# Splitting a unit's last attention tile before or after the next queries, on ScalarE and VectorE

## The reference

```python
q, k, v = layernorm(x) @ Wq, ...                 # 16 query heads, one key head, one value head
sim = jnp.einsum('bhid,bjd->bhij', q, k) + bias  # a null column stands in front
sim = jnp.where(causal_mask, neg, sim)
attn = jax.nn.softmax(sim, axis=-1)
out = jnp.einsum('bhij,bjd->bhid', attn, v)
out = out.transpose(0, 2, 1, 3).reshape(b, n, INNER) @ Wo
x = x + layernorm(out)
```

## Time and profile before

| what | value |
|---|---|
| median of 3 runs | 1648.43 us (1646.07 to 1648.87) |
| the profiled execution, its own time | 1648.25 us |
| span of the profiled execution | 1646.4 us, so 1.85 us lie around it |
| attention, first to last L1210 | about 52 to 1303 us of the span |
| TensorE, VectorE, ScalarE, GpSimd busy | 88%, 85%, 70%, 51% of the span |

### The profile page before, as it was taken

One profiled execution on the slowest core, in us unless ns is written; L12 is line 12 of the kernel. 1 busy time (PEld: TensorE's weight loads), 2 busy tenths in 40 slices (PEclk: granted clock), 3 DMA queues, 4 the chain that ended last, 5 costly groups with the idle time before them and its releaser, 6 DMA issues.

```text
span 1646.4 us, 44788 instructions
## 1 busy us (share of the span) xinstructions
PE 1441.4 (88%) x15551; PEld 1064.3 (65%) x15551; DVE 1406.3 (85%) x3562; ACT 1150.6 (70%) x2957; POOL 838.8 (51%) x1654
## 2 busy tenths in 40 slices
PE   3567778888999999986788899999999989999998
PEld 2445556666777777765666677777777756666665
DVE  5467787899999999987788899999999979888887
ACT  3466667887888888877788888888999723333332
POOL 4768687664554545457775443433232266632222
PEclk8589899999999999999999999999999999999999
DMA  4011121220222213111221212222214001000000
GB/s 147 19 31 55 40 65 53 84 67 33 79 79 91 91 58 125 59 40 33 72 78 53 85 66 72 79 85 91 98 65 144 2 4 43 1 1 1 14 14 26
DMA packets 50754, 96.46 MB, mean 59 GB/s; under 512 B 3732, under 2 KB 27364, under 8 KB 50532
## 3 DMA queue, kind: packets, MB, share of 16 engines
q1 hardware_dynamic: 47988, 92.65, 17.2%
q10 hardware_dynamic: 2544, 0.94, 0.3%
HBM read 91.41 MB, written 2.17 MB: 57 GB/s over the span
## 4 chain that ended last, share of the span: by engine, by line
PE 54%; DVE 21%; issue 7%; ACT 6%; POOL 5%; DVEq 0%; ACTq 0%; POOLq 0%
PE tp L1728 8%; DVE biased L1210 7%; PE sc L1606 5%; DVE p_lo L1309 5%; PE sc L1407 4%; PE sc L1409 4%; PE sc L1408 4%; PE sc L1607 4%; DVE q_a L1242 3%; PE aux L1407 3%; PE op L1407 2%; PE aux L1409 2%; PE aux L1408 2%; PE tp L1407 2%; PE tp L1409 2%
## 5 line engine op out<-in xcount | busy, mean ns | idle before, releaser
L1309 DVE TENSOR_TENSOR p_lo<-tp,p_hi 128x384 f16<-128x384 f32 (+3 forms) x768 | 413.1, 553 | 90.1 <-ACT p_hi L902 80.7
L805 ACT ACTIVATE probs<-biased,neg_max 128x256 f32<-128x256 f32 (+7 forms) x512 | 395.2, 772 | 25.9 <-DVE neg_max L1210 23.7
L1728 PE MATMUL tp<-ident,probs 128*128 128x128 f32 x2304 | 389.7, 278 | 2.4 <-DVE p_lo L1309 1.8
L902 ACT ACTIVATE p_hi<-tp 128x384 f16<-128x384 f32 (+3 forms) x768 | 369.4, 491 | 28.1 <-PE tp L1728 14.3
L1606 PE MATMUL sc<-k_a,q_a 128*128 128x512 f16 (+3 forms) x768 | 254.6, 332 | 90.3 <-DVE neg_max L1210 70.6
L1407 PE MATMUL op<-v_s,p_hi 128*128 128x64 f16 x2304 | 285.2, 194 | 42.7 <-DVE p_lo L1309 27.4
L1728 PEld LDWEIGHTS tp<-ident,probs 128*128 128x128 f32 x2304 | 266.8, 142 | 29.0 <-issue 10.7
L1409 PE MATMUL op<-v_s,p_lo 128*128 128x64 f16 x2304 | 284.2, 194 | 0.0
L1408 PE MATMUL op<-v_s,p_hi 128*128 128x64 f16 x2304 | 284.2, 194 | 0.0
L1407 PEld LDWEIGHTS op<-v_s,p_hi 128*128 128x128 f16 x2304 | 215.6, 98 | 71.7 <-DVE p_lo L1309 48.6
L1607 PE MATMUL sc<-k_b,q_b 128*128 128x512 f16 (+3 forms) x768 | 242.5, 329 | 0.0
(11 more groups left out here) (311 smaller groups left out, 3508.6 us busy)
## 6 DMA issues: line engine op xcount, KB each, us to landing
bias<-rel_table SPq DMA_DIRECT2D x4, 2048.0 KB, 8.0
bias<-in_fside_16xSxS SPq DMA_DIRECT2D x4, 2048.0 KB, 8.6
bias<-rel_table SPq DMA_DIRECT2D x4, 1792.0 KB, 7.8
bias<-in_fside_16xSxS SPq DMA_DIRECT2D x4, 1792.0 KB, 7.1
bias<-rel_table SPq DMA_DIRECT2D x4, 1536.0 KB, 7.6
bias<-in_fside_16xSxS SPq DMA_DIRECT2D x4, 1536.0 KB, 6.7
bias<-rel_table SPq DMA_DIRECT2D x4, 1280.0 KB, 5.8
bias<-in_fside_16xSxS SPq DMA_DIRECT2D x4, 1280.0 KB, 6.5
```

The costliest lines, as they stand in the source:

```text
L805: ac.activation(probs[:, i % 2, 0:w], biased[:, i % 2, 0:w], ACT.Exp, bias=neg_max[:, u % 2, i % HU:i % HU + 1], scale=-1.0, accum_out=row ...
L902: ac.activation(p_hi[:, gi % 4, 0:nb * P], tp[gi % 2][:, 0:nb * P], ACT.Copy)\
L1309: ve.tensor_tensor(p_lo[:, gi % 4, 0:nb * P], tp[gi % 2][:, 0:nb * P], p_hi[:, gi % 4, 0:nb * P], ALU.subtract).then_inc(s["p_lo"], 1)
L1728: last = te.transpose(tp[gi % 2][:, jj * P:(jj + 1) * P], probs[:, n % 2, (j0 + jj) * P:(j0 + jj + 1) * P], ident[:, :])
```

## The change

In a unit's last slot (k = 3) ScalarE and VectorE do the work on the queries of unit m + 2 later. Before, ScalarE's two copies to `q_b` and VectorE's two subtractions into `q_a` stand ahead of the slot's first group of probabilities. Now they stand behind the first group and ahead of what is left of the slot: with one group, behind all of the slot's probabilities; with two, between the two groups. The waits that the instructions carry are the same, and so are the instructions themselves and their number. TensorE's, GpSimd's and SyncE's lists are the same.

```diff
@@ ScalarE, before the slot's groups
-                if k == 3 and 0 <= m + 2 < NU:
-                    u = m + 2
-                    act.wait_ge(s["q_t"], u + 1)
-                    if u >= 2:
-                        act.wait_ge(s["scores"], HU * (u - 1))
-                    for e in range(2):
-                        ac.activation(heads(q_b[0:DH, u % 2, :], e),
-                                      first[e * DH:(e + 1) * DH, 0:UW].rearrange("p (c q) -> p c q", q=P), ACT.Copy)\
-                            .then_inc(s["q_hi"], 1)
+                def queries():
+
+                    u = m + 2
...
@@ ScalarE, in the loop over the slot's groups, behind p_hi of group j
                     if j == 0:
+                        if k == 3 and 0 <= m + 2 < NU:
+                            queries()
                         small()
```

More of the change, by code:

```diff
@@ L838, in _ @@
                         .then_inc(s["q_na"], 1)
+                def queries():
+                    u = m + 2
+                    act.wait_ge(s["q_t"], u + 1)
+                    if u >= 2:
+                        act.wait_ge(s["scores"], HU * (u - 1))
+                    for e in range(2):
+                        ac.activation(heads(q_b[0:DH, u % 2, :], e),
+                                      first[e * DH:(e + 1) * DH, 0:UW].rearrange("p (c q) -> p c q", q=P), ACT.Copy)\
+                            .then_inc(s["q_hi"], 1)
                 def small():
```

## The result

| | before | changed |
|---|---|---|
| median | 1648.25 us (1646.07 to 1648.87, 4 runs) | 1683.39 us (1682.39 to 1683.96, 4 runs) |
| span of the profiled execution | 1646.4 us | 1682.0 us |
| TensorE's granted clock, mean | 0.973 | 0.974 |

The changed kernel is slower: the ratio is 1.0215, 95% interval 1.0197 to 1.0233. The forecast was 1680 us.

The account below looks back on a forecast made before the run. A loop of waits between TensorE, ScalarE and VectorE, not one full engine, was taken to bound the kernel. Long steps 23.5 us plus short steps 8.8 gave 32 us on 1648.25: 1680 us, range 1660 to 1700.

Parts of the forecast that it names:

- The loop in the long steps: Low half, y, TensorE's queue to k = 1's transposes, `p_hi`, VectorE's list, next low half: later y lengthens the unit.
- What was forecast to come back: Unit 114: of y's 0.84 us delay, 0.17 returns at the transposes behind y and 0.09 at the next slot's first scores.
- Its size: Long steps' cost: 56 of 64 units at 0.42 us, 23.5 us in all, bounds 9.5 and 37 us.
- The eight stretches with the rows' statistics: One long unit per step has next rows' statistics before the low half; TensorE already waits at y, so counted as nothing.
- Through which wait it comes back to VectorE: Long steps: the delay returns through VectorE's wait for `p_hi` in k = 1, idle 0.29 us before, as long or longer after.
- the rival of the late queues: Long steps: y's copy on ScalarE delays the next `p_hi`, another 0.3 us, 0.9 a unit at most; about 1698 us; chance 0.14.
- The short steps: Next `biased` up to 0.28 us later, TensorE's scores wait for it: 7 us layer 1, 1.8 layer 0, 8.8 together.
- the quarter: Layer 0's 28 short units taken at a quarter of layer 1's cost, 1.8 us, as their chain holds more than this loop.
- The waits moved as told: Short steps: TensorE's wait for `p_lo` falls near zero, that for `neg_max` grows by about as much.
- the rival of the faster short steps: Short steps: TensorE's 12.9 us wait for `p_lo` paces them and goes, as much again in layer 0; 1632 us; chance 0.08.
- The hidden case: VectorE is the bound and TensorE's slack hides y's delay: 0 to 9.5 us in long steps, about 1653 us; chance 0.12.
- The loop in k = 1: Long steps: VectorE idles 0.29 us for `p_hi`, whose transposes TensorE reaches after y, products, scores and query projection.

Follow-up runs that it names:

- experiment 5: Changed kernel with y and ScalarE's copy of it moved behind the first group's transposes and products in k = 0 of the long steps: 1664.67 us.
- experiment 4: Kernel before with the new order in VectorE's list alone, ScalarE's list in the old order: 1715.0 us, ratio 1.0409.
- e1_long_only: Kernel before with the new order only in slots with two groups (long steps), the old order elsewhere: 1671.12 us, ratio 1.0139.
- experiment 11: Kernel before with the query projection of k = 1 between first transposes and products, only in one-group slots (short steps): 1633.37 us, ratio 0.9916.
- experiment 7: Kernel before with the query projection and ScalarE's copies of it behind the first group's transposes and products in k = 1, everywhere: 1695.4 us.
- experiment 12: Kernel before with the query projection between first transposes and products in k = 1, except in three slots per tile step: 1633.51 us, ratio 0.9918.

## Why the prediction was right, and where it was not

**The loop in the long steps: right.** y starts 0.05 us behind the low half, the wait for `q_a` went from 12.2 to 31.9 us (25 to 35 forecast), and experiment 5, which takes y out of the way and leaves the rest of the change, takes 17 of 24 us back. In unit 114 the low half ends 0.75 us later (0.84 forecast: the copies start 0.11 us before `p_hi` ends by its record, and I had put them behind it, so the low half waits for `p_lo` and not for them). What was forecast to come back came back: on the chain the transposes behind y end at 1189.60 + 0.44 - 31.01 = 1159.03 against 1158.45, 0.58 us later, and the first scores behind them at 1160.22 against 1159.74, 0.48 later. So the two terms are 0.17 and 0.10 (0.17 and 0.09 forecast), and the unit pays 0.75 - 0.27 = 0.48, not the 0.58 of the prediction; that VectorE's next pass behind `o_raw` is 0.58 us later too (1192.20 - 31.01 = 1161.19 against 1160.61) is chance, since one slot on it is 0.49.

**Its size: right, by terms that were each a little off and made up for each other.** Forecast 56 units of 0.42 us and eight of nothing, 23.5; measured 23.7. The eight stretches with the rows' statistics grew too, by 0.19 to 0.40 us, 2.1 in all: the wait for the statistics does not hide the whole of the later low half. Why, no run shows; `p_lo` now stands ahead of the low half there too. The other 56 took 21.6 / 56 = 0.39. Layer 0's long steps cost less than layer 1's (10.5 against 13.2), as said.

**Through which wait it comes back to VectorE: the step that failed.** I expected VectorE's idle time in k = 1 as long or longer. It is shorter, 0.20 us against 0.29, and a new one of 0.33 stands in k = 0, where there was none. It is so in all long steps, not in this unit alone: by the rows of the timeline VectorE's wait for `p_hi` in tile steps 12 to 15 went from 1.1 us (3 times) to 9.4 (25 times) in k = 0 and from 4.9 (20 times) to 1.5 (7 times) in k = 1, and in tile steps 4 to 7 from 0.8 to 7.1 and from 8.5 to 5.8. That is the rival of the late queues: y's copy ends at 1190.03 and the first `p_hi` behind it at about 1190.68, where the rival, with the shift, had 1190.11 and 1190.73. Its mechanism is there and its price is not: the longer wait in k = 0 shortens the one in k = 1, and the unit pays 0.49, not 0.9. Where ScalarE's queue is really late it does cost, as experiment 4 showed.

**The short steps: the sum near, its shares not.** Forecast 7 us in layer 1 and 1.8 in layer 0; measured 6.0 and 4.85. Layer 1's term was priced by unit 78, whose next pass is 0.14 us later and not 0.28, again because the copies overlap the end of `p_hi` (they start at 843.66, 0.10 before it). At 0.14 a unit the sum would have been 4 us, so that it came near is luck; and 1.3 of the 6.0 us lie in tile step 9, which is as much longer in `e1_long_only` with the old order. In layer 0 the quarter was a guess with no row behind it; 3.5 of its 4.85 us lie in tile step 3, most of them in two units (0.89 and 1.39). I can't say from the runs what these two wait for. The waits moved as told, in part: that for `p_lo` fell from 12.9 to 5.4 us and not to near zero, and that for `neg_max` rose by 13.5, more than the other fell. So the rival of the faster short steps is out: its wait did get shorter and the steps longer. The 1.1 us ahead of the first step were in no term, and rightly, by experiment 1.

**The hidden case** is out. VectorE is busy for 88.36 of 93.80 us and had 87.05 of 90.60, TensorE's weight loads for 70.47: the fullest engine got no more to do but 1.3 us of records that overlap less, and the step grew by 3.2. The Trainium skill's rule (Perfetto Trace Analysis, Identifying the Most-Contended Engine), by which the engine with the highest occupancy is the one to look at, points at VectorE here, 94% busy, and doesn't say what set the time. By the measurement, order alone cost 2.15% in the change and gained 0.84% on the kernel before in experiment 11, with no instruction added or removed.

**The loop in k = 1** was the part of my reasoning that no step of the prediction tested, and it was overdrawn. For experiment 7 I expected 11 us from the long steps and 20 from the short ones; experiment 12, where only the projection's place differs, gains 1.0 and 13.2.

## What to carry to other kernels

Where engines take their lists in order and share few PSUM banks, ask of each piece that is moved which bank it frees, who is next in that bank, and what stands behind that one in its own queue; keep the producers' and the consumers' lists in the same order: here moving one alone cost more than moving both. A wait that disappears from the list of waits is no gain until the stage is shorter: read the length of each stage and of each unit in it, since a total that barely moved hid 16.5 us won and 9.3 lost, the latter in three units of eight. A rare piece that shares a bank with a frequent one is to be looked for before the frequent one is moved.

## What the runs showed of the hardware

ScalarE's records of neighbours mostly overlap. The queries' copies, queued behind `p_hi`, start 0.10 to 0.11 us before its recorded end (1186.98 against 1186.49 + 0.60 = 1187.09 in unit 114, 843.66 against 843.38 + 0.38 = 843.76 in unit 78). It is not so for every pair: in the kernel before, `p_hi` behind the same copies starts 0.02 us after their end (1156.00 against 1155.21 + 0.77 = 1155.98), and I can't say why. Where an instruction must wait for another engine it starts behind that one's end, by 0.03 us (`p_lo` at 1187.12 behind `p_hi`) to 0.05 (y). So a list of durations laid end to end can be too long by about 0.1 us at such a step on one engine, and that is most of what made my low half in unit 114 and my next pass in unit 78 too late, by 0.09 and 0.14 us.
